# Three buffers instead of two for the bf16 parts of a convolution, filled three chunks ahead of the products

## The chip, the cores and the metric

The kernel runs on one core of one Trainium2 chip. The metric is the device time of that core in microseconds (us). The core has TensorE (PE in the rows; PEld are its weight loads), VectorE (DVE), ScalarE (ACT), GpSimd (POOL), and SyncE (SP), which here only issues the DMAs. Each engine runs its own instruction list in order; they wait for each other by semaphores.

## What is computed

The program has two stages, one behind the other. The first is an attention block with a residual, the second a depthwise causal convolution with a residual:

```python
def reference(x, cond_2048, L0_cond_Wq, L0_cond_Wo, L1_cond_b):
    x = x + _L0_cond_ref(x, cond_2048, L0_cond_Wq, L0_cond_Wo)      # attention, x is (16, 512, 1024)
    x = x + _L1_cond_ref(x, cond_2048[:, None, :], L1_cond_b)       # y[n] = sum_k w[k] x[n-15+k] + b
    return x
```

In the convolution the 512 rows of x are the positions and the 1024 columns the channels; each channel has 16 taps. All is float32 to the outside.

## The kernel before, in words

The change touches only the second stage, `build_conv` (line 731 on). It turns the convolution into products: 16 positions and 8 channels form the 128 partitions, the data are the stationary operand, and a matrix with the taps on its diagonals (`toep`, bf16) is the moving one. The products are in bf16, so float32 data are first split into three bf16 parts that sum to the value: `first_part` is the value rounded to bf16, `rest` is the float32 remainder, whose upper half serves as the second part, and `last_part` is what is then left.

The work is cut into 64 chunks: 4 rounds of 4 batch entries, 16 chunks in each. For every chunk k:

- ACT writes `first_part` from the input `xin` (`first(k)`, L854), after it has waited until PE is done with the chunk that used this buffer last (`s_bank`).
- DVE makes `rest` (L886) and then `last_part` (L888) in `parts(k)`.
- PE makes two fills of a PSUM bank each. A fill is one matmul of 512 columns that lays down the bias (L944) and 24 matmuls of 128 columns (L950, L951): 4 groups of 8 channels, 3 parts, 2 tap matrices. There are 8 banks.
- ACT copies each fill to `stage` (`evict`, L863).

The three part buffers are taken in turn, `k % 2`. ACT's list is written out by hand: both fills of chunk k are evicted, then `first(k + 2)` is made. Since the list is in order, a `first` that waits holds up the evictions behind it. During the first 8 chunks DVE also writes the second half of `toep` (L880), two instructions behind each `parts`.

SP moves the data. One load of `xin` brings the input of 8 chunks (two DMAs of 2 MB, L796); there are two such buffers, and 8 loads in all. After every 4 chunks SP stores `stage` (four DMAs of 512 KB, L802), which has two buffers as well. SP's list behind the beginning is store, store, load, over and over: the load that refills a half of `xin` stands behind the second of two stores. I call the moment at which this second store is issued T0: it comes when the last fill of chunk 7 (15, 23, ...) has been evicted, and the load that follows it brings chunks 16 to 23 (24 to 31, ...). A load is first waited for by the `first` of the first chunk that it brings (`s_in`).

Of the kernel before, what the change touches and what calls it, by code (L numbers as in the profile page):

```python
# [6 lines left out]
F32 = mybir.dt.float32  # L7
F32R = mybir.dt.float32r
BF16 = mybir.dt.bfloat16
ACT = mybir.ActivationFunctionType  # L10
ALU = mybir.AluOpType
# [4 lines left out]
P = 128  # L16
# [702 lines left out]
SLOTS = (NC + 1) * NB  # L719
TC = 8  # L720
# [2 lines left out]
PER_BANK = 4  # L723
FILLS = TC // PER_BANK
NBANK = 8
SC = 32
STAGES = TG // SC
PER_STAGE = SC // TC


def build_conv(nc, x1, taps_in, bias, out):
# [6 lines left out]
    with ExitStack() as ctx:  # L738
        def sb(name, shape, dt):
            return ctx.enter_context(nc.sbuf_tensor(name, shape, dt))  # L740
# [11 lines left out]
        brow = sb("brow", [P, T], BF16)  # L752
        pick = sb("pick", [P, P], BF16)
        xin = sb("xin", [P, 2, SLOTS, TH], F32)
        rest = sb("rest", [P, 2, SLOTS, TC], F32)
        first_part = sb("first_part", [P, 2, SLOTS, TC], BF16)
        last_part = sb("last_part", [P, 2, SLOTS, TC], BF16)
        stage = sb("stage", [P, 2, CH, SC * NG], F32)
        taps_f32 = stage[:, 0].rearrange("p l t -> p (l t)")[:, 0:CH * TG].rearrange("p (n l) -> p n l", l=CH)
        braw = stage[:, 1].rearrange("p l t -> p (l t)")[:, 0:T]  # L760
        brest = stage[:, 1].rearrange("p l t -> p (l t)")[:, T:2 * T]
        acc = [ctx.enter_context(nc.psum_tensor(f"acc{k}", [P, HALF], F32)) for k in range(NBANK)]

# [8 lines left out]
        s_first = sem("s_first")  # L772
        s_rest = sem("s_rest")
        s_last = sem("s_last")
        s_bank = sem("s_bank")
# [4 lines left out]
        ALL = ROUNDS * CHUNKS  # L780
# [3 lines left out]
        def upper(a):  # L784

            return a.bitcast(BF16)[..., 1::2]

        @block.sync
        def _(sp):
# [8 lines left out]
            def store(k):  # L798
                sp.wait_ge(s_res, FILLS * PER_STAGE * (k + 1))
                r, q = k // STAGES, k % STAGES  # L800
                for b in range(NB):
                    sp.dma_start(out_rows[r * NB + b][:, :, q * SC * NG:(q + 1) * SC * NG],  # L802
                                 stage[b:P:NB, k % 2]).then_inc(s_out[k % 2], 16)
# [14 lines left out]
        def raw(k):  # L818
            q = k % CHUNKS
            at = q % PER_LOAD * TC  # L820
            return xin[:, q // PER_LOAD, :, at:at + TC]
# [24 lines left out]
        @block.scalar  # L846
        def _(act):
            def first(k):
                if k % PER_LOAD == 0:
                    act.wait_ge(s_in[k // PER_LOAD % 2], 32 * (k // CHUNKS + 1))  # L850
                    act.wait_ge(s_zero, 2)
                if k >= 2:
                    act.wait_ge(s_bank, FILLS * (k - 1))
                act.activation(first_part[:, k % 2], raw(k), ACT.Copy).then_inc(s_first, 1)  # L854

            def evict(n):
                k, f = n // FILLS, n % FILLS
                s, part = k // PER_STAGE, k % PER_STAGE
                if part == 0 and f == 0 and s >= 2:
                    act.wait_ge(s_out[s % 2], 16 * NB * (s // 2))  # L860
                to = (part * TC + f * PER_BANK) * NG
                act.wait_ge(s_bank, n + 1)
                act.activation(stage[:, s % 2, :, to:to + PER_BANK * NG].rearrange("p l (n g) -> p l n g", g=NG),  # L863
                               acc[n % NBANK][:].rearrange("p (n g l) -> p l n g", n=PER_BANK, l=CH),
                               ACT.Copy).then_inc(s_res, 1)

            first(0)
            first(1)
            for k in range(ALL):
                for f in range(FILLS):  # L870
                    evict(FILLS * k + f)
                if k + 2 < ALL:
                    first(k + 2)

        @block.vector
        def _(dve):
            def place_taps(h, g):

                for w in range(2):
                    dve.tensor_scalar(toep[:, w, h * TH:(h + 1) * TH, g * CH:(g + 1) * CH],  # L880
                                      taps[:, w, h * TH:(h + 1) * TH, :], group[:, g:g + 1], None,
                                      ALU.mult).then_inc(s_toep, 1)

            def parts(k):
                dve.wait_ge(s_first, k + 1)
                dve.tensor_tensor(rest[:, k % 2], raw(k), first_part[:, k % 2], ALU.subtract).then_inc(s_rest, 1)  # L886
                dve.wait_ge(s_rest, k + 1)
                dve.tensor_tensor(last_part[:, k % 2], rest[:, k % 2], upper(rest[:, k % 2]), ALU.subtract).then_inc(s_last, 1)  # L888

            def bias_rows():  # L890
                dve.wait_ge(s_bias, 16 * len(ROWS))
                for row in ROWS[1:]:
                    one = slice(row, row + 1)
                    dve.tensor_tensor(brest[one], braw[one], upper(braw[one]), ALU.subtract).then_inc(s_brow, 1)  # L894
                dve.tensor_copy(brow[0:1, :], upper(braw[0:1])).then_inc(s_brow, 1)  # L895
                dve.wait_ge(s_brow, 8)
                one = slice(ROWS[1], ROWS[1] + 1)
                dve.tensor_copy(brow[one, :], upper(brest[one])).then_inc(s_brow, 1)  # L898
                one = slice(ROWS[2], ROWS[2] + 1)
                dve.tensor_tensor(brow[one, :], brest[one], upper(brest[one]), ALU.subtract).then_inc(s_brow, 1)  # L900

            dve.memset(pick[:], 0.0).then_inc(s_brow, 1)
            dve.memset(brow[:], 0.0).then_inc(s_brow, 1)
            dve.wait_ge(s_brow, 2)
            for row in ROWS:
                dve.memset(pick[row:row + 1, :], 1.0).then_inc(s_brow, 1)
            dve.wait_ge(s_keep, 7)
            dve.tensor_reduce(own[:], eye[:].rearrange("p (g l) -> p l g", l=CH), AX.X, ALU.max).then_inc(s_own, 1)
            dve.tensor_reduce(tri[:], keep[:].rearrange("p w (g l) -> p w l g", l=CH), AX.X, ALU.max).then_inc(s_own, 1)
            dve.tensor_reduce(group[:], eye[:].rearrange("p (g l) -> p g l", l=CH), AX.X, ALU.max).then_inc(s_own, 1)  # L910
            dve.wait_ge(s_own, 3)
            dve.wait_ge(s_taps, 16)
            own_b = own[:].unsqueeze(1).to_broadcast([P, TG, CH])
            dve.tensor_tensor(taps_f32, taps_f32, own_b, ALU.add).then_inc(s_own, 1)  # L914
            dve.wait_ge(s_own, 4)
            for w in range(2):
                tri_b = tri[:, w:w + 1, :].to_broadcast([P, TG, CH])
                dve.tensor_tensor(taps[:, w], taps_f32, tri_b, ALU.mult).then_inc(s_own, 1)  # L918
            dve.wait_ge(s_own, 6)
            for g in range(NG):  # L920
                place_taps(0, g)
            bias_rows()
            for k in range(ALL):
                parts(k)
                if k < PER_LOAD:
                    place_taps(1, k)

        @block.tensor
        def _(pe):
            for k in range(ALL):  # L930
                q = k % CHUNKS
                if k == 0:
                    pe.wait_ge(s_brow, 10)
                if k % PER_LOAD == 0 and k < CHUNKS:
                    pe.wait_ge(s_toep, 2 * NG * (k // PER_LOAD + 1))
                pe.wait_ge(s_last, k + 1)
                slabs = (first_part[:, k % 2], upper(rest[:, k % 2]), last_part[:, k % 2])
                for f in range(FILLS):
                    at = FILLS * k + f
                    if at >= NBANK:  # L940
                        pe.wait_ge(s_res, at + 1 - NBANK)
                    n0 = (q * TC + f * PER_BANK) * NG
                    extra = brow[:, n0:n0 + PER_BANK * NG].unsqueeze(2).to_broadcast([P, PER_BANK * NG, CH])
                    pe.matmul(acc[at % NBANK][:], pick[:], extra, start=True, stop=False, skip_group_check=True)  # L944
                    for i in range(PER_BANK):
                        j = f * PER_BANK + i
                        o = acc[at % NBANK][:, i * P:(i + 1) * P]
                        t0, t1 = toep[:, 0, q * TC + j, :], toep[:, 1, q * TC + j, :]
                        for slab in slabs:
                            pe.matmul(o, slab[:, NB:SLOTS, j], t0, start=False, stop=False, skip_group_check=True)  # L950
                            last = pe.matmul(o, slab[:, 0:P, j], t1, start=False, stop=slab is slabs[-1],  # L951
                                             skip_group_check=True)
                    last.then_inc(s_bank, 1)
# [46 lines left out]
```

## Time and profile before

| | |
|---|---|
| median of 3 runs | 4359.39 us (4355.31 to 4359.48) |
| the profiled execution | 4359.21 us |
| its span in the trace | 4357.5 us |
| the attention stage | from the start to about 4070 us |
| the convolution | from about 4071 us to the end; its products from 4097.7 us |
| PE busy over the whole span | 95% |

The span is what the trace covers, from the first instruction to the last; the profiled execution's own time is 1.7 us longer. The page of the profile is almost wholly about the attention stage, so for this change the trace has to be asked about the last 290 us alone.

### The profile page before, as it was taken

The numbers are of one execution on the slowest core, as the hardware profiler recorded it, in microseconds if no ns is written. First come the engines' busy times: TensorE is split into PE (matmuls) and PEld (weight loads), VectorE is DVE, ScalarE is ACT, GpSimd is POOL, SyncE is SP. The second block draws the span as 40 slices with busy tenths as digits, with TensorE's granted clock in tenths as the row PEclk, the third lists the DMA queues.
The fourth block names the chain that finished last, engine by engine and source line by source line (L and its number), as shares of the span: only waits on it lengthen the run. The fifth ranks groups of instructions, "written<-read, shape, count | busy, mean of one in ns | idle before, by whom it ended". The sixth has DMA issues, their size and how long they took to land. (4 is left out here: it accounts for less than half of the span.)

```text
span 4357.5 us, 56947 instructions
## 1 busy us (share of the span) xinstructions
PE 4157.0 (95%) x18688; PEld 2984.3 (68%) x18688; DVE 2496.9 (57%) x2259; ACT 2851.1 (65%) x3905; POOL 2605.3 (60%) x1044
## 2 busy tenths in 40 slices
PE   6999999999999999999999999999999999999698
PEld 4776767677676767767676766767676776766487
DVE  4664556556565655556565556555555565655665
ACT  3775767667575766767576766757676675757255
POOL 3775757667575756757575666757676675757000
PEclk8999999999999999999999999999999999999899
DMA  3322333332332333242233323233333323321586
GB/s 97 83 69 65 82 83 92 74 83 69 80 81 68 88 75 90 64 103 69 59 88 83 88 63 92 69 68 82 79 92 74 83 69 82 79 71 47 160 282 217
DMA packets 285135, 385.34 MB, mean 88 GB/s; under 512 B 148915, under 2 KB 216115, under 8 KB 284726
## 3 DMA queue, kind: packets, MB, share of 16 engines
q1 hardware_dynamic: 284854, 381.57, 34.2%
q8 instruction: 179, 2.93, 0.3%
q14 instruction: 102, 0.84, 0.1%
HBM read 112.28 MB, written 67.11 MB: 41 GB/s over the span
## 5 line engine op out<-in xcount | busy, mean ns | idle before, releaser
L579 POOL TENSOR_TENSOR plo<-p,phi 128x1024 fp32r<-128x1024 f32 x1024 | 2600.0, 2551 | 1421.6 <-ACT phi L529 1411.0
L622 DVE TENSOR_REDUCE mrow<-misc 128x1 f32<-128x1024 f32 x1024 | 1214.3, 1217 | 1083.4 <-PE misc L373 1079.1
L527 ACT ACTIVATE p<-sc 128x512 f32<-128x512 f32 x2048 | 1110.6, 594 | 846.5 <-PE sc L410 623.7
L423 PE MATMUL pv<-phi,val 128*128 128x512 f32 x4096 | 1138.9, 400 | 41.4 <-issue 41.4
L529 ACT ACTIVATE phi<-p 128x1024 fp32r<-128x1024 f32 x1024 | 1086.1, 1061 | 32.5
L409 PE MATMUL sc<-quer,keys 128*128 128x512 f32 x2048 | 919.0, 449 | 24.4 <-issue 19.4
L423 PEld LDWEIGHTS pv<-phi,val 128*128 128x128 f32 x4096 | 768.8, 189 | 249.8 <-issue 76.1
L410 PE MATMUL sc<-quer,keys 96*128 96x512 f32 x2048 | 815.6, 398 | 0.0
L427 PE MATMUL pv<-plo,val 128*128 128x512 f32 x2048 | 648.4, 398 | 0.7 <-POOL plo L579 0.7
L373 PE MATMUL misc<-quer,keys 128*128 128x512 f32 x2048 | 596.8, 399 | 22.7 <-DMA keys<-lo 11.6
L409 PEld LDWEIGHTS sc<-quer,keys 128*128 128x128 f32 x2048 | 387.3, 189 | 202.1 <-issue 77.0
L652 DVE RECIPROCAL den<-den 128x128 f32<-128x128 f32 x512 | 468.2, 934 | 49.1 <-ACT den L516 22.4
L395 PE MATMUL misc<-ct,wo 128*128 128x512 f32 x1024 | 464.4, 597 | 30.8 <-DVE mrow L622 20.7
L360 PE MATMUL misc<-xb,wq 128*128 128x512 f32 x1024 | 463.4, 596 | 17.0 <-DMA wo<-woT 15.6
L373 PEld LDWEIGHTS misc<-quer,keys 128*128 128x128 f32 x2048 | 385.6, 191 | 136.9 <-ACTq L496 22.0
L410 PEld LDWEIGHTS sc<-quer,keys 96*128 96x128 f32 x2048 | 388.2, 190 | 114.9 <-issue 48.1
L427 PEld LDWEIGHTS pv<-plo,val 128*128 128x128 f32 x2048 | 380.9, 188 | 103.8 <-POOL plo L579 13.6
L667 DVE TENSOR_TENSOR xo<-misc,xo 128x512 f32<-128x512 f32 x128 | 88.5, 691 | 469.6 <-PE misc L395 469.6
L395 PEld LDWEIGHTS misc<-ct,wo 128*128 128x128 f32 x1024 | 191.1, 190 | 241.7 <-issue 205.6
L360 PEld LDWEIGHTS misc<-xb,wq 128*128 128x128 f32 x1024 | 195.1, 191 | 215.3 <-issue 186.2
L493 ACT ACTIVATE q<-misc 128x512 f32<-128x512 f32 x128 | 76.6, 598 | 336.6 <-PE misc L360 336.6
L658 DVE TENSOR_TENSOR ct<-ca,den 128x1024 f32<-128x1024 f32 x64 | 206.3, 3223 | 13.9 <-DVE mneg L642 13.7
(66 smaller groups left out, 2646.7 us busy)
## 6 DMA issues: line engine op xcount, KB each, us to landing
keys<-hi SPq DMA_DIRECT2D x256, 256.0 KB, 3.1
quer<-mhi SPq DMA_DIRECT2D x256, 256.0 KB, 4.4
xb<-x SPq DMA_DIRECT2D x16, 2048.0 KB, 8.7
keys<-lo SPq DMA_DIRECT2D x128, 256.0 KB, 4.9
quer<-mlo SPq DMA_DIRECT2D x128, 256.0 KB, 3.8
xo<-x SPq DMA_DIRECT2D x64, 512.0 KB, 3.8
x<-xo SPq DMA_DIRECT2D x64, 512.0 KB, 5.1
xin<-x SPq DMA_DIRECT2D x16, 2048.0 KB, 14.3
```

Of the source, the lines that this page charges most:

```text
L360: last = pe.matmul(out, wq[:, k, np_ * P:(np_ + 1) * P], xb[:, k, half(h)], start=(k == 0), stop=(k == DT - 1))
L373: last = pe.matmul(out[:, half(h)], keys[:, k, tok(q)], quer[:, k, half(h)], start=True, stop=True)
L395: last = pe.matmul(out, wo[:, k, m * P:(m + 1) * P], ct[:, k, half(h)], start=(k == 0), stop=(k == PAIRS - 1))
L409: pe.matmul(sc[:, h, :], keys[:, k, tok(t)], quer[:, k, half(h)], start=True, stop=False)
L410: pe.matmul(sc[:, h, :], keys2[:, i, tok(t)], quer2[:, i, half(h)], start=False, stop=True).then_inc(s_sc, 1)
L423: pe.matmul(pv[:, half(h)], val[:, i, t, part, :], phi[:, t % NPHI, half(h)], start=(t == 0 and part == 0), stop=False)
L427: last = pe.matmul(pv[:, half(h)], val[:, i, t, 0, :], plo[:, t % NPLO, half(h)], start=False, stop=(t == KT - 1))
L527: act.activation(p32[:, t % NP32, half(h)], sc[:, h, :], ACT.Exp, scale=SCALE).then_inc(s_p32, 1)
L529: act.activation(phi[:, t % NPHI, :], p32[:, t % NP32, :], ACT.Copy).then_inc(s_phi, 1)
L579: pool.tensor_tensor(plo[:, t % NPLO, :], p32[:, t % NP32, :], phi[:, t % NPHI, :].bitcast(F32), ALU.subtract).then_inc(s_plo, 1)
L622: reduced = dve.tensor_reduce(mrow[:, q:q + 1], misc[:, k, :], AX.X, ALU.max)
L652: dve.reciprocal(d, d).then_inc(s_rden, 1)
```

## The change

All three part buffers get a third slot, taken in turn as `k % 3`. ACT makes the first part of chunks 0, 1 and 2 ahead of everything, and from then on `first(k + 3)` behind the evictions of chunk k, where `first(k + 2)` stood. The wait of `first(k)` is for the end of chunk k - 3 instead of k - 2. Amount and form of all instructions stay the same.

```diff
+NPART = 3
...
-        rest = sb("rest", [P, 2, SLOTS, TC], F32)
-        first_part = sb("first_part", [P, 2, SLOTS, TC], BF16)
-        last_part = sb("last_part", [P, 2, SLOTS, TC], BF16)
+        rest = sb("rest", [P, NPART, SLOTS, TC], F32)
+        first_part = sb("first_part", [P, NPART, SLOTS, TC], BF16)
+        last_part = sb("last_part", [P, NPART, SLOTS, TC], BF16)
...
-                if k >= 2:
-                    act.wait_ge(s_bank, FILLS * (k - 1))
-                act.activation(first_part[:, k % 2], raw(k), ACT.Copy).then_inc(s_first, 1)
+                if k >= NPART:
+                    act.wait_ge(s_bank, FILLS * (k - NPART + 1))
+                act.activation(first_part[:, k % NPART], raw(k), ACT.Copy).then_inc(s_first, 1)
...
-            first(0)
-            first(1)
+            for k in range(NPART):
+                first(k)
             for k in range(ALL):
                 for f in range(FILLS):
                     evict(FILLS * k + f)
-                if k + 2 < ALL:
-                    first(k + 2)
+                if k + NPART < ALL:
+                    first(k + NPART)
```

DVE's and PE's lists change only in the buffer that they name (`k % NPART` for `k % 2`). On ACT the first rows of the convolution stood like this before (L854 is `first`, L863 is `evict`; "waits" names the semaphores):

```order
L846 UNCONDITIONAL_BRANCH [waits barrier_Pool_Activation_PE_DVE_SP_release]
L854 ACTIVATE first_part<-xin 128x1056 [waits s_zero,s_in0]
L854 ACTIVATE first_part<-xin 128x1056
L863 ACTIVATE stage<-acc 128x16x32 [waits s_bank] x2
L854 ACTIVATE first_part<-xin 128x1056 [waits s_bank]
L863 ACTIVATE stage<-acc 128x16x32 [waits s_bank] x2
```

In the changed kernel, whose lines stand one further down (L855, L864), they are:

```order
L847 UNCONDITIONAL_BRANCH [waits barrier_Pool_Activation_PE_DVE_SP_release]
L855 ACTIVATE first_part<-xin 128x1056 [waits s_zero,s_in0]
L855 ACTIVATE first_part<-xin 128x1056 x2
L864 ACTIVATE stage<-acc 128x16x32 [waits s_bank] x2
L855 ACTIVATE first_part<-xin 128x1056 [waits s_bank]
L864 ACTIVATE stage<-acc 128x16x32 [waits s_bank] x2
```

The third `first` has moved ahead of the first two evictions, and every later one has moved up by one chunk.

The second place is where ACT first needs a load that SP issued behind a store (`s_in0` for the second time, chunk 16). `s_out1` marks the eviction that begins chunk 12. Before:

```order
L863 ACTIVATE stage<-acc 128x16x32 [waits s_bank,s_out1]
L863 ACTIVATE stage<-acc 128x16x32 [waits s_bank]
L854 ACTIVATE first_part<-xin 128x1056 [waits s_bank]
L863 ACTIVATE stage<-acc 128x16x32 [waits s_bank] x2
L854 ACTIVATE first_part<-xin 128x1056 [waits s_bank]
L863 ACTIVATE stage<-acc 128x16x32 [waits s_bank] x2
L854 ACTIVATE first_part<-xin 128x1056 [waits s_bank,s_zero,s_in0]
L863 ACTIVATE stage<-acc 128x16x32 [waits s_bank] x2
```

And in the changed kernel:

```order
L864 ACTIVATE stage<-acc 128x16x32 [waits s_bank,s_out1]
L864 ACTIVATE stage<-acc 128x16x32 [waits s_bank]
L855 ACTIVATE first_part<-xin 128x1056 [waits s_bank]
L864 ACTIVATE stage<-acc 128x16x32 [waits s_bank] x2
L855 ACTIVATE first_part<-xin 128x1056 [waits s_bank,s_zero,s_in0]
L864 ACTIVATE stage<-acc 128x16x32 [waits s_bank] x2
```

The wait for the load stood behind the evictions of chunk 14 and stands now behind those of chunk 13, with the evictions of chunks 14 and 15 queued behind it.

## Rows read from the trace of the kernel before

**Rows 1.** The page, span in 40 slices: PE busy, granted TensorE clock, in tenths

```profile
PE   6999999999999999999999999999999999999698
PEclk8999999999999999999999999999999999999899
```

**Rows 2.** Two stretches: busy PE, PEld, DVE, ACT, POOL; clock, DMA share, GB/s

```profile
4224.03:4239.70 15.67, 14.32 (x201) 13.20 (x202) 10.07 (x8) 8.71 (x13) 0.00 (x0) 1.00 0.96 306
4239.70:4245.90 6.20, 6.11 (x88) 5.68 (x89) 3.59 (x3) 3.72 (x5) 0.00 (x0) 1.00 1.09 358
```

**Rows 3.** Chain of waits, 4208 to 4225 us: start, length, what

```profile
4211.97 0.39 PE acc L944
...
4215.58 0.60 ACT stage L863
4216.18 0.99 ACT first_part L854
4217.19 1.27 DVE rest L886
4218.48 1.27 DVE last_part L888
4219.80 0.39 PE acc L944
```

**Rows 4.** Timeline of one chunk and the start of the next

```profile
4208.25 1.08 ACT L854 ACTIVATE first_part<-xin 128x1056 bf16<-128x1056 f32 x1
4208.37 0.39 PE L944 MATMUL acc<-brow,pick 128*128 128x512 bf16 x1 [0.65 <-DVE last_part L888]
...
4210.07 0.38 PE L944 MATMUL acc<-brow,pick 128*128 128x512 bf16 x1
...
4211.96 0.60 ACT L863 ACTIVATE stage<-acc 128x512 f32<-128x512 f32 x1 [1.03 <-PE acc L951]
...
4212.46 1.07 ACT L854 ACTIVATE first_part<-xin 128x1056 bf16<-128x1056 f32 x1
```

**Rows 5.** Timeline, PE: bias matmuls of chunks 0, 1 and 63

```profile
4097.70 0.59 PE L944 MATMUL acc<-brow,pick 128*128 128x512 bf16 x1 [32.26 <-DVE last_part L888]
...
4100.65 0.38 PE L944 MATMUL acc<-brow,pick 128*128 128x512 bf16 x1
...
4102.35 0.38 PE L944 MATMUL acc<-brow,pick 128*128 128x512 bf16 x1
...
4345.00 0.39 PE L944 MATMUL acc<-brow,pick 128*128 128x512 bf16 x1 [0.21 <-DVE last_part L888]
4346.72 0.38 PE L944 MATMUL acc<-brow,pick 128*128 128x512 bf16 x1
```

**Rows 6.** Timeline, DVE in the first chunks

```profile
4099.55 1.26 DVE L888 TENSOR_TENSOR last_part<-rest 128x1056 bf16<-128x1056 f32 x1
...
4104.15 1.26 DVE L886 TENSOR_TENSOR rest<-xin,first_part 128x1056 f32<-128x1056 f32 x1 [2.55 <-ACT first_part L854]
...
4107.57 1.26 DVE L886 TENSOR_TENSOR rest<-xin,first_part 128x1056 f32<-128x1056 f32 x1
```

**Rows 7.** Timeline, SP's DMA issues over one round of store, load, store

```profile
4224.04 3.69 SPq L802 DMA_DIRECT2D out<-stage  x4
4227.77 5.86 SPq L796 DMA_DIRECT2D xin<-x  x2
4239.69 16.86 SPq L802 DMA_DIRECT2D out<-stage  x6
```

**Rows 8.** Line L796, two of the six such loads: issue starts, and issue to landing

```profile
L796 SPq DMA_DIRECT2D xin<-x x2: 1354/2908/4461, 4227.8 to 4229.2; - x2
DMA to landing us min/median/max: 11.9/14.3/16.7
...
DMA to landing us min/median/max: 11.5/14.3/17.0
```

**Rows 9.** Timeline, ACT: the first part that needs that load

```profile
4251.53 1.08 ACT L854 ACTIVATE first_part<-xin 128x1056 bf16<-128x1056 f32 x1
```

More of the change, by code:

```diff
@@ L885, in parts @@
                 dve.wait_ge(s_first, k + 1)
-                dve.tensor_tensor(rest[:, k % 2], raw(k), first_part[:, k % 2], ALU.subtract).then_inc(s_rest, 1)
+                dve.tensor_tensor(rest[:, k % NPART], raw(k), first_part[:, k % NPART], ALU.subtract).then_inc(s_rest, 1)
                 dve.wait_ge(s_rest, k + 1)
-                dve.tensor_tensor(last_part[:, k % 2], rest[:, k % 2], upper(rest[:, k % 2]), ALU.subtract).then_inc(s_last, 1)
+                dve.tensor_tensor(last_part[:, k % NPART], rest[:, k % NPART], upper(rest[:, k % NPART]), ALU.subtract).then_inc(s_last, 1)
             def bias_rows():
@@ L936, in _ @@
                 pe.wait_ge(s_last, k + 1)
-                slabs = (first_part[:, k % 2], upper(rest[:, k % 2]), last_part[:, k % 2])
+                slabs = (first_part[:, k % NPART], upper(rest[:, k % NPART]), last_part[:, k % NPART])
                 for f in range(FILLS):
```

## The prediction

> **What bounds the kernel now.** I read the page first, then the busy times of the last stretch, then the chain of waits there, and last the timeline engine by engine. The page says that PE is busy all through the attention stage at full clock [rows 1]; nothing of that stage is touched, so the change can only win or lose time in the last 290 us. There the busy times are no help at first sight: PE 14.32 of 15.67 us, with clock 1.00 [rows 2]. But ends of matmuls are modelled and overlap, so I go by starts.
>
> The chain shows a loop. A chunk's products begin at 4211.97, its second fill is evicted at 4215.58, ACT makes the first part into the freed buffer, DVE makes the two others, and the products from the same buffer begin at 4219.80 [rows 3]. The loop takes 4219.80 - 4211.97 = 7.83 us, and with two buffers two chunks pass in it, one every 3.91 us. What PE itself needs is less. From one bias matmul to the next, with nothing waited for in between, it takes 1.70 us (4208.37 to 4210.07 [rows 4]; 4100.65 to 4102.35, across a chunk's edge [rows 5]) or 1.72 us (4345.00 to 4346.72 [rows 5]). Two fills are a chunk: 3.40 to 3.44 us, and I take 3.41, since two of the three read 1.70. So PE stands still for 0.50 us of each 3.91. This is latency of the loop and no lack of an engine: DVE needs 2 x 1.29 = 2.58 us per chunk and ACT two evictions of 0.60 and one first part of 1.08, 2.28 us [rows 3, 4].
>
> **What the change removes.** With three buffers, three chunks pass in one loop. The loop itself stays 7.83 us if nothing in it waits, so it would allow 2.61 us per chunk. That is below PE's 3.41, which becomes the bound. Parts that are ready early cost nothing; the third `first` at the beginning (1.08 us on ACT) lies before the first eviction, when ACT is idle.
>
> Chunks 0 and 1 don't wait for a buffer, so their times stay. Chunk 1 starts at 4102.35 and chunk 63 at 4345.00 [rows 5]: 62 steps in 242.65 us, 3.914 each. At 3.41 they take 211.4 us. **The gain is 31.2 us.** The tail behind chunk 63 (its fills, the last store) has the same instructions; the last load is long done by then, so I leave it. With a fill of 1.70 us the gain would be 31.9 us, with 1.72 us 29.4 us; these are the bounds for the pace.
>
> **DVE in the first chunks.** There it carries the tap matrix as well and begins a new `rest` every 4107.57 - 4104.15 = 3.42 us [rows 6], 0.01 more than PE. It starts with a lead: chunk 1's last part is done at 4099.55 + 1.26 = 4100.81, 1.5 us before PE wants it at 4102.35 [rows 5, 6]. Seven times 0.01 don't use it up. Cost: nothing.
>
> **The load.** This is the one wait that the change brings closer, by two ways: the `first` that needs the load moves up a chunk, and the chunks get shorter. I count from T0, which is 4224.04 in [rows 7]. The load's second DMA is issued at 4229.2 and lands 16.7 us later [rows 8], at T0 + 21.9; with the longest of the six such loads, 17.0 us [rows 8], it would be T0 + 22.2. ACT took the first part that needs it at 4251.53 [rows 9], T0 + 27.5: 5.6 us to spare.
>
> Now the same point at the new pace. An eviction of a second fill starts 3.59 us after its chunk (4208.37 to 4211.96), and the `first` behind it 0.50 us later [rows 4]. T0 is that eviction's end for chunk 7, so it lies 3.59 + 0.60 - 3.41 = 0.8 us after the start of chunk 8. ACT comes to `first(16)` behind chunk 13's evictions: 5 x 3.41 + 3.59 + 0.50 = 21.1 us after the start of chunk 8, T0 + 20.3. It will stand there for 1.6 to 1.9 us, with the evictions of chunk 14 behind it. Does PE feel this? Chunk 16 can start at the earliest 8 x 3.41 = 27.3 us after chunk 8, at T0 + 26.5. From `first` to products it takes 3.72 us (4208.25 to 4211.97 [rows 3, 4]). So `first(16)` may start as late as T0 + 22.8, and the load lands 0.6 to 0.9 us ahead of that. Queued behind are chunk 14's two evictions: PE has 8 banks, four chunks, so it doesn't wait for them. What is late next is `first(17)`, at about T0 + 24.4, where T0 + 26.2 would do. ACT's 2.28 us per chunk against 3.41 let it catch up in two chunks. Cost: nothing, if the load lands as now. Six loads stand at this place (those issued from T0 on); the other two, issued before the products, land far ahead of their chunks.
>
> **Will it land as now?** Between T0 and the even store's issue (4239.69) 15.67 us x 306 GB/s = 4.80 MB moved, and until the load's landing another 6.20 x 358 = 2.22 MB [rows 2], 7.02 MB together. Store and load are 6.29 MB. So 0.7 MB of the even store had moved by the time the load was reported. Either the store's packets ran between those of the load, or the load's data were in already and its semaphore came some 2 us late. At the new pace the even store is issued 2.0 us earlier (4 x 0.50), at T0 + 13.6. In the second reading nothing changes. In the first, the load loses 0.72/2.22, a third, of each us that the store is out: some 1.0 us more, landing at T0 + 22.9 to 23.2, a stall of 0.1 to 0.4 us, six times, 1 to 3 us. I take the second: at 4239.69 the load had 1.49 MB left, which at 358 GB/s are 4.2 us, and the landing came after 6.2.
>
> The Trainium skill speaks to this in "DMA: Bandwidth & Descriptors", section on queues, rings and completion order: each DMA engine takes the descriptors of one queue in ring order. Its part on the anatomy of a DMA puts most of about 2 us of fixed cost on the receipt of the last write. That is the second reading, and the surplus of 2 us in the trace agrees. By the page the sum stays at 31.2 us; by an even sharing it would be 28 to 30.
>
> **Sum.** The profiled execution took 4359.21 us (span 4357.5); minus 31.2 this is 4328.0. The median shown is 0.2 us above it, so 4328 for the median as well.
>
> **The rivals.**
> *The loads come late.* If the even store, 2.10 MB at 350 GB/s, went wholly ahead of what is left of the load, the load would land 6.0 us later, at T0 + 27.9: 5.1 us beyond T0 + 22.8. Every us beyond that point stalls PE by a us, six times: 31 us, and the time would be 4359, no change. A part of it is likelier than all: 1 to 10 us, 4329 to 4338. For it: the DMA engines move 8.39 MB per 8 chunks, which at 340 to 358 GB/s take 23.4 to 24.7 us of a round that shrinks from 31.3 to 27.3, so queues grow on any disturbance. Against: still 2.6 us are left, and the odd store issued at T0 meets an empty queue as now.
> *The DMA engines become the bound.* They would need over 27.3 us for 8.39 MB, so less than 307 GB/s on the average of a round. The rows show 306 over the first 15.67 us with its slow start in it, but 358 behind [rows 2], so I give this little. At 300 GB/s a round would be 28.0 us, 0.7 x 7 = 5 us lost, 4333.
> *The change doesn't do what it says.* If PE's 0.50 us were not the loop but the wait for something else, the time would stay at 4359. The idle time in [rows 4] before the bias matmul is put down to `last_part`, and the chain closes over ACT and DVE; I see nothing for this rival.
> *Slower: the clock falls under the denser products.* PE would run without a gap for 211 us. At the lower of its two levels, 1.2 GHz, a fill takes longer: chunk 0's first fill ran from 4097.70 and its second began at 4100.65 [rows 5], 2.95 us instead of 1.70, 1.25 us more. To end over 8.7 us slower than before, 31.2 + 8.7 = 39.9 us must be lost: 32 fills, a quarter of all, at the lower level. Against it: PE was busy for 0.9 and more of nearly every slice of the attention stage and was granted 0.9 and more of the clock there [rows 1]. A time of 4370 for 34 such fills.
>
> **How the numbers follow.** The sum as worked out: 0.76. Loads late by a part, or DMAs as the bound, 4329 to 4345: 0.19. No change, by a store wholly ahead or the loop read wrongly: 0.03. Slower by the clock: 0.02. A difference of 0.2%, 8.7 us, is about what can be told from none here; so faster 0.95, same 0.03, slower 0.02. The range takes the pace's bounds (4327.3 to 4330), the spread of the runs shown downwards (4355.31 is 4.1 us below the median, so 4323), and upwards the late loads of up to 10 us: 4323 to 4338.
>
> **What the changed profile would show.** Bias matmuls at chunk starts 3.40 to 3.44 us apart; chunk 63 starting 31 us earlier, at about 4314; PE's wait for `last_part` gone from all chunks but the first. DVE's waits for `first_part` stay, since DVE is no longer late but early. A new wait of ACT, first part for the DMA of `xin`, six times 1.6 to 1.9 us, 9 to 11 us in total: if it is missing, my count of the load's slack is wrong; if it is over 2.5 us at a time, PE stalls there too, and the six stalls are what the gain lacks. Wrong would be all of it if the fills themselves took over 1.75 us, which would mean that the denser traffic on SBUF slows PE.

## The result and the profile after

The changed kernel took 4326.9 us (median of 6 runs, 4325.65 to 4329.07) against 4359.08 us for the kernel before in the same comparison (6 runs, 4355.31 to 4360.9). The ratio is 0.9928, 95% interval 0.9915 to 0.9941: 32 us less, where 31.2 were forecast. The profiled execution took 4327.44 us.

The page of the profile after: the span, the busy line, and granted clock in 40 slices. The share of PE rises by one point; the page says no more than that, which is why the reading has to go on in the last 250 us.

```profile
span 4325.7 us, 56947 instructions
...
PE 4148.8 (96%) x18688; PEld 2982.9 (69%) x18688; DVE 2496.5 (58%) x2259; ACT 2850.3 (66%) x3905; POOL 2604.2 (60%) x1044
...
PEclk8999999999999999999999999999999999999799
```

PE's bias matmuls, from the timeline, at the edge of chunks 0 and 1 and at chunk 63 (answering to [rows 5]):

```profile
4096.87 0.59 PE L945 MATMUL acc<-brow,pick 128*128 128x512 bf16 x1 [32.30 <-DVE last_part L889]
4099.82 0.63 PE L945 MATMUL acc<-brow,pick 128*128 128x512 bf16 x1
4102.03 0.38 PE L945 MATMUL acc<-brow,pick 128*128 128x512 bf16 x1
4103.73 0.38 PE L945 MATMUL acc<-brow,pick 128*128 128x512 bf16 x1
...
4313.25 0.38 PE L945 MATMUL acc<-brow,pick 128*128 128x512 bf16 x1
```

Chunk 1 starts at 4102.03 and chunk 63 at 4313.25: 62 steps in 211.22 us, 3.407 each, where 211.4 were forecast and 242.65 were needed before. No row behind the first shows a wait. The span became 31.8 us shorter: 31.4 in these steps, 0.3 because chunk 1 happened to start earlier.

The waits in the convolution, all engines (line waited for, us in total, times, longest):

```profile
ACT stage L864 <- PE acc L952: 78.2, 77, 9.4
DVE rest L887 <- ACT first_part L855: 47.3, 46, 2.7
...
PE acc L945 <- DVE last_part L889: 32.3, 1, 32.3
ACT first_part L855 <- DMA xin<-x: 9.1, 6, 1.7
```

PE's wait for the last part is the one ahead of chunk 0, and that is all. DVE still waits for the first part, but for less (80.0 us before) and without PE noticing. In its place stands the wait that the prediction had named: ACT waits for a load, six times, 9.1 us in total. SP's issues in one such round and ACT's timeline at the load show it closely. SP first:

```profile
4181.21 3.70 SPq L803 DMA_DIRECT2D out<-stage  x4
4184.95 5.90 SPq L797 DMA_DIRECT2D xin<-x  x2
4194.83 1.97 SPq L803 DMA_DIRECT2D out<-stage  x1
```

The even store is issued 13.6 us behind T0, as worked out. ACT in the round before:

```profile
4173.77 0.60 ACT L864 ACTIVATE stage<-acc 128x512 f32<-128x512 f32 x1 [1.10 <-PE acc L952]
4176.09 1.09 ACT L855 ACTIVATE first_part<-xin 128x1056 bf16<-128x1056 f32 x1 [1.72 <-DMA xin<-x]
4177.08 1.07 ACT L864 ACTIVATE stage<-acc 128x512 f32<-128x512 f32 x2
4178.03 1.08 ACT L855 ACTIVATE first_part<-xin 128x1056 bf16<-128x1056 f32 x1
```

Two evictions had queued up behind the waiting `first` and follow it at once (4177.08, x2); the next `first` comes 1.94 us behind the late one, and ACT has caught up. PE's rows meanwhile keep their 1.70 us.

That load's row of line L797 says where it landed: issued at 4159.1, 17.0 us.

```profile
L797 SPq DMA_DIRECT2D xin<-x x2: 1343/3089/4835, 4157.7 to 4159.1; - x2
DMA to landing us min/median/max: 12.1/14.5/17.0
```

All six of these loads took 16.4 to 17.0 us from the issue of their second DMA to the landing, exactly the span of the six before (two of them, 16.7 and 17.0, are in [rows 8]), although the even store now follows 2 us sooner. The bytes say the same. Here are the stretches from T0 to the even store's issue, and from there to the landing at 4202.90 (the last two numbers are DMA share and GB/s, as in [rows 2]):

```profile
4181.21:4194.83 13.62, 13.62 (x203) 13.03 (x202) 10.91 (x9) 8.69 (x13) 0.00 (x0) 1.00 0.94 300
4194.83:4202.90 8.07, 8.07 (x121) 7.70 (x120) 5.17 (x5) 4.32 (x7) 0.00 (x0) 1.00 1.09 354
```

13.62 us at 300 GB/s are 4.09 MB, so 2.20 MB of the load were left when the even store was issued. At 354 GB/s they need 6.2 us, and the landing came after 8.07: 1.9 us of surplus, against 2.0 before. So it was the second reading: the store doesn't delay the load ahead of it.

### The profile page after: what moved, and what is told of

It is laid out like the page before. It is cut to its first block and busy times, and to the rows that moved or that the text cites. A ratio compares the mean times of both kernels' runs of the same rounds, so it can differ in the third digit from the quotient of the medians.

```text
span 4325.7 us, 56947 instructions
## 1 busy us (share of the span) xinstructions
PE 4148.8 (96%) x18688; PEld 2982.9 (69%) x18688; DVE 2496.5 (58%) x2259; ACT 2850.3 (66%) x3905; POOL 2604.2 (60%) x1044
## 5 line engine op out<-in xcount | busy, mean ns | idle before, releaser
L373 PE MATMUL misc<-quer,keys 128*128 128x512 f32 x2048 | 596.2, 399 | 22.6 <-DMA keys<-lo 11.6
L360 PE MATMUL misc<-xb,wq 128*128 128x512 f32 x1024 | 463.4, 596 | 17.3 <-DMA wo<-woT 15.9
```

The lines of the kernel that those rows point to most:

```text
L360: last = pe.matmul(out, wq[:, k, np_ * P:(np_ + 1) * P], xb[:, k, half(h)], start=(k == 0), stop=(k == DT - 1))
L373: last = pe.matmul(out[:, half(h)], keys[:, k, tok(q)], quer[:, k, half(h)], start=True, stop=True)
```

## The experiments

To compare runs beyond the attention stage, which varies by a few us from run to run, I use the stretch from ACT's first to its last eviction; it is the starts "from ... to" in the rows of the eviction's line. Before:

```profile
L863 ACT ACTIVATE stage<-acc x128: 597/600/610, 4100.9 to 4348.6; 128x512 f32<-128x512 f32 x128
```

and after:

```profile
L864 ACT ACTIVATE stage<-acc x128: 580/601/608, 4100.1 to 4316.8; 128x512 f32<-128x512 f32 x128
```

that is 247.7 and 216.7 us. The table gives this stretch for every run (for c2 up to DVE's last eviction), beside the median time and that of the kernel before in the same comparison.

| run | median us | before | stretch us |
|---|---|---|---|
| a1_buffers_only | 4360.45 | 4360.92 | 248.6 |
| a2_two_buffers_first_early | 4344.97 | 4360.92 | 233.7 |
| a3_four_buffers | 4332.79 | 4360.92 | 219.9 |
| a4_load_early | 4328.30 | 4360.92 | 216.4 |
| b1_load_late | 4350.32 | 4359.46 | 236.5 |
| b2_before_load_late | 4360.48 | 4359.46 | 248.5 |
| b3_no_bias | 4314.85 | 4359.46 | 206.0 |
| b4_no_bias_load_early | 4309.10 | 4359.46 | 197.4 |
| c1_pool_bias | 4405.96 | 4359.31 | 297.9 |
| d1_four_buffers_load_early | 4329.35 | 4359.37 | 216.6 |
| d2_pool_beside | 4377.09 | 4359.37 | 266.8 |
| c2_dve_adds_quarter | 4319.60 | 4359.37 | 209.9 |

### Is it the buffers or the order?

a1: the buffers alone.

```diff
-            for k in range(NPART):
+            for k in range(2):
                 first(k)
...
-                if k + NPART < ALL:
-                    first(k + NPART)
+                if k + 2 < ALL:
+                    first(k + 2)
```

> Three buffers, but ACT still makes the first part only two chunks ahead, behind the evictions of chunk k. Theory (the loop of products, eviction, three parts sets the pace, and its length in chunks is set by where first stands in ACT's list): the first part of chunk k + 2 still can't begin before chunk k is evicted, the loop stays 7.83 us for two chunks, 3.91 us per chunk, and the time stays at 4359 us. Rival (the wait for a free buffer is the limit, so a third buffer is enough by itself): 3.41 us per chunk, 4327 us.

The ratio is 1.0000 (0.9990 to 1.0009). A third buffer that nobody fills ahead is worth nothing that can be measured here.

a2: two buffers, and of the order only a part.

```diff
-                for f in range(FILLS):
-                    evict(FILLS * k + f)
+                evict(FILLS * k)
                 if k + 2 < ALL:
                     first(k + 2)
+                evict(FILLS * k + 1)
```

> Two buffers as before, but the first part of chunk k + 2 stands between the two evictions of chunk k instead of behind both. Theory (loop): the 0.50 us between the start of the second eviction and that of the first part leave the loop, which becomes 7.33 us for two chunks, 3.67 per chunk; 62 steps of 0.25 us less are 15 us: 4344 us. Rival (ACT's order doesn't matter with two buffers, only their number): 4359 us.

Ratio 0.9965 (0.9950 to 0.9979), and the stretch is 14.0 us shorter, where 15 were expected. Both together say what the loop is: products, what stands ahead of `first` in ACT's list, three parts. PE's first bias matmuls of three chunks in its timeline (7.43 us from 4211.47 to 4218.90, where the loop took 7.83 before [rows 3]):

```profile
4211.47 0.39 PE L944 MATMUL acc<-brow,pick 128*128 128x512 bf16 x1 [0.27 <-DVE last_part L888]
...
4214.97 0.39 PE L944 MATMUL acc<-brow,pick 128*128 128x512 bf16 x1
...
4218.90 0.39 PE L944 MATMUL acc<-brow,pick 128*128 128x512 bf16 x1 [0.36 <-DVE last_part L888]
```

### How near is the load?

a3: `NPART = 4`. a4: the load ahead of the second store.

```diff
             for k in range(ROUNDS * STAGES):
-                store(k)
                 if k % 2 == 1 and k // 2 + 2 < 2 * ROUNDS:
+                    sp.wait_ge(s_last, PER_LOAD * (k // 2 + 1))
                     load(k // 2 + 2)
+                store(k)
```

> Four buffers, four chunks ahead. Theory: PE is already the bound, so no gain. ACT comes to the first part that needs a load at T0 + 16.9 instead of T0 + 20.3 and stands there for about 5.0 us, six times, some 28 to 30 us in total, with more evictions queued behind; the last of them ends about 0.6 us late, which moves the next store and load. Time 4327 to 4330 us. Rival (more run-ahead gives PE more reserve and hides the late load): 4327 us and ACT's wait for the load not above the 1.6 us of three buffers.

> The changed kernel with each load issued as soon as DVE has made the last part that reads the old input, ahead of the second store instead of behind it. Theory: the six waits of ACT for a load (9.1 us in total) disappear, and since PE never felt them the time stays at 4327 us within 2 us. Rival (those waits cost PE something that the sum over starts hides): up to 9 us faster, 4318 us.

Four buffers are slower than three: 4332.79 us against the 4328.30 of a4, taken in the same comparison, and no run of one lies among those of the other. That is also 2.8 us above the range expected. (Against the changed kernel itself the intervals of the ratios overlap, 0.9920 to 0.9953 and 0.9915 to 0.9941; there the trace has to tell.) ACT's waits in the convolution:

```profile
ACT first_part L855 <- DMA xin<-x: 30.0, 5, 6.7
ACT first_part L855 <- PE acc L952: 6.2, 1, 6.2
```

The wait of 6.2 us put down to PE is the sixth of the same kind (4209.06, where the load landed). ACT comes a chunk earlier to the same landing, so it stands longer, and the evictions behind it pile up: six, later eight that follow each other without a wait for PE. T0 itself is late then, and with it the next load. From one T0 to the next it took 4159.20 - 4131.30 = 27.9 us instead of 27.3:

```profile
4131.30 3.71 SPq L803 DMA_DIRECT2D out<-stage  x4
...
4159.20 3.70 SPq L803 DMA_DIRECT2D out<-stage  x4
```

The waits grow with the rounds, from 4.9 us to 6.7, and from the third of these loads on PE feels it: before chunks 32, 40, 48 and 56 it waits 0.35, 0.66, 0.83 and 0.43 us for the last part, and the fill ahead of each wait lasts, from bias matmul to bias matmul, 2.23, 2.54, 2.71 and 2.31 us instead of 1.70. That is 3.0 us together, and the stretch is 3.2 us longer than with three buffers, a little over the 0 to 3 expected. In a4 ACT has no wait for a load at all, and the stretch is 216.4 us against 216.7: the 9.1 us of waiting in the changed kernel cost PE nothing.

d1 puts both together, four buffers and the early load:

> Four buffers, with each load ahead of the second store. Theory (all that four buffers lost against three came from the load, behind which evictions, store and next load queued up): ACT's waits for the load are gone or far below 5 us, PE never waits after the first chunk, and the time is that of three buffers, 4327 us. Rival (the fourth buffer costs by itself, by its place in memory or by ACT's order): 4331 us or more again.

It has no wait for a load, and the stretch is 216.6 us. So the fourth buffer costs nothing by itself; what it lost came from the load. (The median, 4329.35, is 2.4 us above the time expected and can't be told from that of three buffers.)

b1 and b2 ask from the other side: each load is held back by six fills, in the changed kernel and in the one before.

```diff
                 if k % 2 == 1 and k // 2 + 2 < 2 * ROUNDS:
+                    sp.wait_ge(s_res, FILLS * PER_STAGE * (k + 1) + 6)
                     load(k // 2 + 2)
```

> The changed kernel with each load held back until six more fills are evicted, 10.2 us after T0. Theory (deadline at T0 + 22.8): alone in the queue its second DMA lands some 14 to 15.4 us after the issue, at T0 + 24.2 to 25.6, which is 1.4 to 2.8 us too late; six loads: 8 to 17 us, 4335 to 4344 us, with PE waiting for the last part once per load. Rival (the eight banks and the parts made ahead cover it): 4327 us.

> The kernel before with the same delay of six fills, 11.7 us at its pace. Theory: the load lands at T0 + 25.7 to 27.1, and ACT comes for it only at T0 + 27.5, so nothing changes: 4359 us, no wait of ACT for the load. Rival (the loads were near the path before, too): 4365 us or more.

The same delay cost the kernel before nothing (ratio 1.0004, 0.9994 to 1.0013) and the changed one 20 us of stretch; its 4350.32 us are 6 us above the range expected. SP's timeline has T0 at 4127.18 and the load at 4137.39; the second DMA, at 4137.8, landed 14.6 us later, at T0 + 25.2, 2.4 us behind the deadline of T0 + 22.8. The waits of the convolution:

```profile
PE acc L946 <- DVE last_part L890: 47.0, 7, 32.1
ACT first_part L856 <- DMA xin<-x: 29.5, 6, 5.1
```

Without the first 32.1 us PE waited 14.9 us at six places, 2.5 each. That bears out the deadline. But the stretch grew by 19.8 us, 5 more than PE waited. The clock has most of them. These are stretches around two of the loads, with the granted clock third from the end:

```profile
4182.00:4185.75 3.75, 1.59 (x26) 1.45 (x24) 2.58 (x3) 3.73 (x6) 0.00 (x0) 1.00 1.05 368
4185.75:4190.00 4.25, 4.25 (x41) 3.91 (x41) 4.18 (x4) 1.85 (x3) 0.00 (x0) 0.60 0.70 239
...
4214.50:4217.20 2.70, 0.13 (x3) 0.01 (x1) 2.58 (x3) 2.70 (x6) 0.00 (x0) 0.97 0.94 332
4217.20:4222.00 4.80, 4.80 (x51) 4.36 (x52) 4.73 (x4) 1.84 (x3) 0.00 (x0) 0.66 0.72 248
```

PE stood for 2.2 and 2.6 us, and behind that the clock was at the lower level, 1.2 GHz, for part of the next 5 us. It fell so behind three of the six stalls; at the third, which ended at 4278.77, it was granted 0.85 and 0.81 over two stretches of 5 us (4275 to 4285). The length of the stall alone doesn't decide it: the clock fell behind the shortest of the six (2.2 us) and stayed at 1.00 behind the longest, 2.70 us, which is the first row below. The price can be read from the starts of the bias matmuls. The two fills behind each of those three stalls took 4.2 us more than 1.70 each, six fills in all; the first fill behind the stall at 4217 took 2.96. The six fills with a stall in them took 15.9 us more. Together this is 20.1 us, and the stretch grew by 19.8.

```profile
4248.68 0.39 PE L946 MATMUL acc<-brow,pick 128*128 128x512 bf16 x1 [2.70 <-DVE last_part L890]
...
4217.19 0.61 PE L946 MATMUL acc<-brow,pick 128*128 128x512 bf16 x1 [2.57 <-DVE last_part L890]
4220.15 0.52 PE L946 MATMUL acc<-brow,pick 128*128 128x512 bf16 x1
4221.99 0.38 PE L946 MATMUL acc<-brow,pick 128*128 128x512 bf16 x1
```

### What bounds it next?

b3 leaves out the bias matmuls, so that the output lacks the bias; b4 does the same with the early load.

```diff
-                    pe.matmul(acc[at % NBANK][:], pick[:], extra, start=True, stop=False, skip_group_check=True)
...
-                            pe.matmul(o, slab[:, NB:SLOTS, j], t0, start=False, stop=False, skip_group_check=True)
+                            pe.matmul(o, slab[:, NB:SLOTS, j], t0, start=slab is slabs[0], stop=False, skip_group_check=True)
```

> The changed kernel without the bias matmuls, so that the bias is left out of the output: PE needs about 0.215 us less per fill, 2.97 us per chunk. Theory: the load now is the limit. The first part may start at T0 + 19.2 at the latest and the load lands at T0 + 21.9: a stall of 2.7 us, six times. 62 x 0.44 = 27 us are gained and 16 given back: 4316 us. Rival (PE alone is the bound): 4300 us. Second rival (the DMA engines, 24.7 us per 8 chunks, are the bound, more than the load's place): 4306 us.

> The same without the bias, with the load ahead of the second store. Theory (the load's place was the limit in the run above): PE at 2.97 us per chunk needs 23.8 us per 8 chunks and the DMA engines 24 to 24.7, so 4300 to 4306 us, without a wait of ACT for a load. Rival (the DMA engines are so full that the place doesn't matter): 4316 us as in the run above.

b3 is where the first theory put it (4316 expected, 4314.85 measured), but not wholly by the way expected, and that the sum still comes out is in part luck. Leaving out the first, PE waited 11.6 us at six places, 1.9 on the average where 2.7 were expected; and over two stretches of 5 us the granted clock was 0.66, where four fills took 2.31, 2.15, 2.27 and 2.18 us instead of 1.49, another 3 us. This is the wait, and the first of the two stretches (the other is 4279 to 4284 us):

```profile
PE acc L949 <- DVE last_part L889: 44.1, 7, 32.5
```

```profile
4200.00:4205.00 5.00, 4.76 (x53) 4.77 (x54) 4.93 (x5) 2.20 (x5) 0.00 (x0) 0.66 0.69 234
```

The chain of its execution closes over the load in every round, which is a row like this six times:

```profile
4151.11 1.03 SPq L803
4152.19 1.34 SPq L797
4153.57 16.67 DMA xin<-x
4170.26 1.09 ACT first_part L855
```

In b4 the load is out of the chain and the time falls to 4309.10, 3 us above the range expected. The waits have a new one, which I had not foreseen: ACT's eviction for the store that must free `stage`. The chain now goes in every round over such a store, some 8.0 us from issue to landing. The rate in 40 slices of the stretch from 4140 to 4260 us, and the DMA queue's row for it:

```profile
ACT stage L865 <- DMA out<-stage: 21.6, 6, 3.7
```

```profile
GB/s 384 273 234 357 349 349 369 379 383 366 122 369 347 349 357 379 384 380 161 325 351 352 348 374 384 383 284 190 361 353 348 361 383 387 377 108 368 354 351 355
...
q1 hardware_dynamic: 39693, 39.89, 99.0%
```

Its loads are issued every 25.1 us, 8.39 MB each round, 334 GB/s. The DMA engines are nearly full, but that they are the limit isn't shown: once in a round the rate falls to 108 to 190 GB/s for a slice of 3 us, and elsewhere it reaches 387; the share of time, too, stands above 1 in other stretches (1.09 in [rows 2]), so that 99.0% is no ceiling. b4's stretch is 19 us below that of the changed kernel. Whether fewer bytes or a third `stage` buffer would bring it lower, no run shows.

### Two versions for use

c1 lets GpSimd, idle in this stage, add the bias; the bias matmuls are gone and the load is early.

```diff
+            for k in range(ALL):
...
+                pool.wait_ge(s_res, FILLS * (k + 1))
+                pool.tensor_tensor(part, part, bias_all[:, q * TC * NG:(q + 1) * TC * NG].unsqueeze(1).to_broadcast([P, CH, TC * NG]),
+                                   ALU.add).then_inc(s_add, 1)
```

> A version for use: three buffers, loads ahead of the second store, no bias matmuls; the bias is laid out over all partitions once and GpSimd, idle in this stage, adds it in float32 to each chunk in stage before the store. Theory: GpSimd needs about 2.55 us per chunk (its 128x1024 operation in the attention stage), below 2.97; the bias rows that DVE made ahead of the first parts (4089.8 to 4095.0) go, so the products start 5 us earlier; the last addition comes 2.5 us behind the last eviction. 4298 to 4304 us. Rival (GpSimd and DVE slow each other, so that DVE's 2.58 us per chunk grow beyond PE's need): 4315 us or more.

It is 47 us slower than the kernel before (ratio 1.0107, 1.0090 to 1.0123) and some 100 us above what was expected; the rival named the mechanism but not its size. Groups of instructions of its convolution:

```profile
L891 DVE TENSOR_TENSOR rest<-xin,first_part 128x1056 f32<-128x1056 f32 x64 | 201.1, 3142 | 0.2 <-ACT first_part L859 0.2
L848 POOL TENSOR_TENSOR stage<-stage,bias_all 128x1024 f32<-128x1024 f32 x64 | 188.2, 2942 | 133.8 <-ACT stage L868 133.7
L893 DVE TENSOR_TENSOR last_part<-rest 128x1056 bf16<-128x1056 f32 x64 | 88.9, 1389 | 2.2
```

`rest` takes 3.14 us on the average instead of 1.26, and DVE is now the bound with some 4.7 us per chunk. To see whether this is the two engines or the flow through `stage`, d2 is the changed kernel with an addition on GpSimd that touches only memory of its own:

```diff
+            for k in range(ALL):
+                pool.wait_ge(s_bank, FILLS * (k + 1))
+                pool.wait_ge(s_spare, k + 1)
+                pool.tensor_tensor(spare[:, 1], spare[:, 0], spare[:, 0], ALU.add).then_inc(s_spare, 1)
```

> The changed kernel, and beside it GpSimd adds 128x1024 float32 in memory that nobody else uses, once per chunk as soon as its products are done. Theory (GpSimd and DVE block each other while both read operands from memory): DVE's rest takes 3.1 to 3.5 us instead of 1.26, last_part nearly as before, 4.7 us per chunk, so about 4405 us. Rival (it was the additions to stage that the stores and the buffers waited for): DVE stays at 2.58 us per chunk and the time at 4327 us.

It is the engines: nobody waits for this work, yet `rest` takes 2.74 us on the average and the time is 4377.09, 50 us more than without it. The mean, and the timelines of DVE and GpSimd for one chunk:

```profile
L894 DVE TENSOR_TENSOR rest<-xin,first_part 128x1056 f32<-128x1056 f32 x64 | 175.3, 2739 | 0.0
```

```profile
4203.26 1.26 DVE L896 TENSOR_TENSOR last_part<-rest 128x1056 bf16<-128x1056 f32 x1
4204.43 2.95 DVE L894 TENSOR_TENSOR rest<-xin,first_part 128x1056 f32<-128x1056 f32 x1
```

```profile
4204.05 2.22 POOL L852 TENSOR_TENSOR spare<-spare 128x1024 f32<-128x1024 f32 x1 [1.94 <-PE acc L959]
```

GpSimd begins at 4204.05 and ends at 4206.27; `rest`, begun at 4204.43, ends at 4207.38, 1.1 us later, about its own length alone. So it stood until GpSimd had finished. The Trainium skill says this in "SBUF — State Buffer", section on who interferes with whom: a DVE instruction with two inputs in SBUF and a GpSimd instruction that reads SBUF exclude each other for a whole instruction. The rows agree. It also fits the size, which came out smaller than the 4405 us expected: in c1 GpSimd's operation at 4178.82 took 2.97 us, and the `rest` of 4179.45, 3.46 us long, ended again 1.1 us behind it; here GpSimd's own operation is only 2.2 us long.

c2 leaves GpSimd alone. DVE evicts every fourth fill and adds the bias on the way, and PE leaves out the bias matmul of that fill; the load is early.

```diff
+                if k >= NPART and (k - NPART) % 2 == 1:
+                    evict_add(k - NPART)
                 parts(k)
...
-                    pe.matmul(acc[at % NBANK][:], pick[:], extra, start=True, stop=False, skip_group_check=True)
+                    if at % 4 != 3:
+                        pe.matmul(acc[at % NBANK][:], pick[:], extra, start=True, stop=False, skip_group_check=True)
```

> A version for use: three buffers, loads ahead of the second store, and every fourth fill is evicted by DVE, which adds the bias in float32 on the way, so that PE needs no bias matmul for it; GpSimd stays idle. Theory: PE saves 0.215 us in every second chunk, 0.11 per chunk, 6.7 us in all; DVE needs 2.58 + 0.35 = 2.93 us per chunk, below PE's 3.30, ACT less than before: 4320 to 4322 us. Rival (the eviction stands in DVE's list where it waits for PE and makes the parts late): 4327 us or more.

4319.60 us, ratio 0.9910 (0.9897 to 0.9924), the fastest of those that compute the whole result. The new operation of DVE reads PSUM and one operand in SBUF:

```profile
L907 DVE TENSOR_TENSOR stage<-acc,bias_all x32: 681/683/692, 4106.3 to 4308.9; 128x512 f32<-128x512 f32 x32
```

From the first eviction of ACT (4099.0) to the last one of DVE (4308.9) it is 209.9 us, 6.8 less than in the changed kernel, where 6.7 were expected. The intervals of the two ratios still overlap, so that it beats the changed kernel rests on the trace more than on the times. Its times (4317.87 to 4321.54) do lie below all of d1 (4325.38 to 4332.55) in the same comparison. ACT now waits six times for a store that must free `stage`, 9.7 us in total, which PE doesn't feel.

## Why the prediction was right, point by point

- **The loop as the bound, 7.83 us for two chunks.** Right. a1 shows that the buffers alone don't touch it, a2 that 0.4 to 0.5 us taken out of it come back as 14.0 us.
- **PE as the next bound at 3.41 us per chunk, a gain of 31.2 us.** Right: 3.407, and 31.4 us over the 62 steps. The rivals of a lower clock under dense products and of DMA engines as the bound did not come: the clock was 1.00 from chunk 1 to chunk 63, and a round took 27.3 us. In b4 the DMA engines carried the same bytes in 25.1 us a round.
- **DVE in the first chunks costs nothing.** Right: PE has no wait behind chunk 0.
- **ACT waits six times for the load, 1.6 to 1.9 us each, 9 to 11 us in all, and PE doesn't feel it.** Right: six times, 1.3 to 1.7 us, 9.1 in all, and a4 without the waits is equally fast. The waits were a little shorter than worked out.
- **The deadline at T0 + 22.8.** Borne out by b1, where a landing at T0 + 25.2 (2.4 us late) stalled PE by 2.5 us a time, and by b2, where the same delay was free in the kernel before.
- **The even store doesn't delay the load.** Right: 17.0 us from issue to landing with the store 2 us sooner.
- **What I had too low** is the price of a late load: not only the stall, but behind three of six stalls in b1 also a fill or two at the lower clock, 4 us over its six loads. In the rival of late loads every us counted as one. This made no difference here, as no load was late.

Of the 31.8 us in the profiled execution 0.3 are no work of the change, and the medians differ by 32.2; both lie within the spread of the runs around the 31.2 forecast. Open is why the clock fell behind some stalls of 2.2 to 2.7 us and not behind others, and what bounds b4.

## What to carry to other kernels

Buffers are worth what the order of the lists lets them hold: count the loop that refills one, in us, divide by the number of buffers that are really filled ahead, and compare with the busiest engine. Once that engine is the bound, further run-ahead only moves waits for inputs earlier, in front of other work of an in-order engine, so check each load's landing against the latest time at which it may be used. Before work is put on an idle GpSimd, look at what DVE reads at that time.

## What the runs showed of the hardware

- With GpSimd adding in SBUF, a DVE subtraction with both inputs in SBUF took 2.74 us on the average instead of 1.26 (d2) and 3.14 us (c1); `last_part`, with the same kinds of operands but mostly out of GpSimd's time, only 1.28 to 1.39. Of DVE's 16 writes of `toep` in d2, with one tensor as input, some took up to 2.12 us, where all took 0.48 in the changed kernel.
- Stalls of PE of 2.2 and 2.6 us were followed by the lower clock, three of six in b1: 0.60 and 0.66 granted over the next 4 to 5 us, and a fill of 2.96 us instead of 1.70. One of 2.70 us was not.
- In b4 the packets of the DMA queue took 99.0% of the 16 engines' time over 120 us, at 334 GB/s, with loads and stores of 1 KB pieces mixed.
- A store issued behind a load on the same queue, and 2 us sooner than before, left the load's landing where it was, 16.4 to 17.0 us from its issue.
